# Expert loop of a decoder layer: how far ahead of a block's output each engine works on the blocks behind it

## What is computed

```
probs = softmax(x @ gate_w);  w, sel = top_k(probs, 8);  w = w / sum(w)
xg = rows of x, gathered per expert, at most C = 1024 rows each
g = xg @ w_gate[e];  u = xg @ w_up[e]            # 256 -> 96
y = (silu(g) * u) @ w_down[e]                    # 96 -> 256
out[token] += w_slot * y                         # 8 experts per token
```

## Time and profile before

| what | value |
|---|---|
| median of 3 runs | 627.1 us (624.79 to 627.71) |
| span of the profiled execution | 719.4 us |
| mean granted TensorE clock | 0.915 of full |
| busy PE / weight loads / DVE / ACT / POOL | 78 / 58 / 51 / 46 / 54 % |
| first down product to last | 390.5 to 657.6 us |

### The profile page before, as it was taken

How to read it: one execution, slowest core, us unless ns; L and a number is a source line. 1 busy time by engine, 2 the same in 40 slices (tenths; PEclk the granted TensorE clock), 3 DMA queues, 4 the chain that set the end, 5 groups by cost and what they waited for, 6 DMA issues and landing times.

```text
span 719.4 us, 17476 instructions
## 1 busy us (share of the span) xinstructions
PE 563.9 (78%) x5097; PEld 414.4 (58%) x5098; DVE 368.4 (51%) x1527; ACT 330.1 (46%) x1204; POOL 390.5 (54%) x599
## 2 busy tenths in 40 slices
PE   3768787888878888888306889988998888985995
PEld 2445454544555554444105777777777776774884
DVE  1537566666677566666402444444444444443453
ACT  2445555455455455456003555555555554553012
POOL 5443445545544455545551666766666666665432
PEclk9789999999999899999556999999999999998899
DMA  9999996111111111112285554555555454554994
GB/s 206 277 275 365 342 339 231 69 59 73 68 50 64 55 73 73 65 66 74 99 308 182 155 165 150 160 156 167 152 164 159 143 157 142 164 160 148 425 418 145
DMA packets 83069, 121.31 MB, mean 169 GB/s; under 512 B 13779, under 2 KB 72669, under 8 KB 80992
## 3 DMA queue, kind: packets, MB, share of 16 engines
q1 hardware_dynamic: 64128, 78.46, 36.3%
q0 software_dynamic: 14016, 38.44, 14.7%
q10 hardware_dynamic: 4896, 4.03, 1.7%
HBM read 56.07 MB, written 69.01 MB: 174 GB/s over the span
## 4 chain that ended last, share of the span: by engine, by line
PE 54%; issue 12%; ACT 12%; DVE 9%; DMA 6%; ACTq 3%; POOL 2%; SPq 1%; another core or an unknown queue 0%; DVEq 0%; POOLq 0%
PE bank L793 14%; PE bank L809 9%; ACT pr L870 7%; PE bank L611 5%; PE bank L785 5%; PE bank L601 4%; PE bank L803 3%; PE bank L661 3%; DMA out<-fin 3%; PE bank L744 2%; DMA wall<-results 2%; DVE nmax L1024 2%; PE bank L619 2%; ACTq L296 1%; DVE tg L1218 1%
## 5 line engine op out<-in xcount | busy, mean ns | idle before, releaser
L556 POOL DMA_INDIRECT results<-ys,wcol x152 | 150.1, 988 | 25.8 <-POOL pscrap L545 22.0
L530 POOL DMA_INDIRECT queues<-x,xidx x128 | 129.1, 1009 | 36.9 <-issue 36.5
L793 PE MATMUL bank<-wall,xtT 128*128 x616 | 127.1, 330 | 0.7 <-issue 0.7
L870 ACT ACTIVATE pr<-bank,nmax 128x128 f32<-128x128 f32 x256 | 90.9, 370 | 29.1 <-DVE nmax L1024 29.1
L1218 DVE SCALAR_TENSOR_TENSOR tg<-th,bank 128x96 f32<-128x96 f32 x154 | 39.1, 254 | 125.3 <-ACT th L957 96.9
L793 PEld LDWEIGHTS bank<-wall,xtT 128*128 128x128 f32 x616 | 98.4, 194 | 1.4 <-issue 1.3
L963 ACT ACTIVATE ys<-bank,wcol 128x256 f32<-128x256 f32 x152 | 71.9, 473 | 54.6 <-PE bank L809 36.6
L809 PE MATMUL bank<-wall,hT 96*128 x304 | 94.5, 392 | 0.0
L785 PE MATMUL bank<-ident,xt 128*128 128x128 f32 x310 | 63.3, 286 | 35.4 <-DMA xt<-queues 24.1
L785 PEld LDWEIGHTS bank<-ident,xt 128*128 128x128 f32 x310 | 59.0, 197 | 49.9 <-DMA xt<-queues 25.1
L876 ACT COPY prT<-bank 128x512 f32<-128x512 f32 x64 | 38.5, 601 | 88.9 <-PE bank L611 86.2
(11 more groups left out here) (178 smaller groups left out, 947.2 us busy)
## 6 DMA issues: line engine op xcount, KB each, us to landing
xt<-queues SPq DMA_DIRECT2D x162, 160.0 KB
results<-zeros SPq DMA_DIRECT2D x16, 1024.0 KB
wall<-results SPq DMA_DIRECT2D x16, 1024.0 KB, 12.7
queues<-zeros SPq DMA_DIRECT2D x32, 160.0 KB, 4.9
wall<-in_L_ffn_w_gate SPq DMA_DIRECT2D x4, 768.0 KB
wall<-in_L_ffn_w_up SPq DMA_DIRECT2D x4, 768.0 KB
wall<-in_L_ffn_w_down SPq DMA_DIRECT2D x4, 768.0 KB
results<-ys,wcol POOLq DMA_INDIRECT x152
```

Of the source, the lines that this page charges most:

```text
L530: pool.indirect_dma_start(xg, bass.IndirectOffsetOnAxis(ap=xidx[:, par, k:k + 1], axis=0), x2[:, par, :], None, bounds_check=last_row, oob ...
L556: pool.indirect_dma_start(yr, bass.IndirectOffsetOnAxis(ap=wcol[:, u, 1:2], axis=0), ys[:, u, :], None, bounds_check=last_y, oob_is_err=Fa ...
L793: ins = pe.matmul(bank[2 + u % 2][:, 0:2 * INTER].rearrange("p (g i) -> p g i", g=2), xtT[:, u % 2, kk, :], wall[:, bass.ds(e, GU)].rearrange(
L870: ins = act.activation(pr[:, g % 2, q, :], pS[g % 2][:, q * P:(q + 1) * P], ACT.Exp, bias=nmax[:, 4 * g + q:4 * g + q + 1], accum_out=den[ ...
```

## The change

Every step of the expert loop moves further ahead of the output, and the output's own step moves to the front of the body. For block t the body is now, on PE, `down` of t, `block_T` of t+5, `turn_h` of t+2, `gu` of t+4; on ACT the output of t, the copy of t+5, the tanh of t+4; on DVE the copy of t+2, the weights of t+3, the gate of t+4. Since `down` lags `gu` by four blocks, four offsets are carried from turn to turn. The prologue grows to five `block_T`, four `gu` and two `turn_h`, and PE's first table read moves ahead of the first `block_T`. The first eight offsets read at a turn's top are now for blocks four ahead. DVE reads its table after its first copy of a turn. SP and POOL keep their lists. Buffers and their number are unchanged.

```diff
+HALF = UN // 2
...
-            for t in range(3):
-                block_T(t, t, 0)
-            last_two = [nc.alloc_register(ET.PE, f"last_two{u}") for u in range(2)]
...
-            for t, e in zip((0, 1), neighbours(ET.PE, tab_g[0:1, LEAD:UN], (NE - 1) * WX)):
-                pe.reg_mov(last_two[t], e)
-                gu(t, t, e)
+            for r, v in zip(carried_regs, experts_of(LEAD, HALF)):
+                pe.reg_mov(r, v)
+            block_T(0, 0, 0)
+            block_T(1, 1, 0)
+            gu(0, 0, carried[0])
+            block_T(2, 2, 0)
+            gu(1, 1, carried[1])
+            block_T(3, 3, 0)
             turn_h(0, 0)
+            gu(2, 2, carried[2])
+            block_T(4, 4, 0)
+            turn_h(1, 1)
+            gu(3, 3, carried[3])
             with pe.Fori(0, rounds) as j:
-                e = neighbours(ET.PE, tab_g[0:1, bass.ds(j * UN + UN, UN)], (NE - 1) * WX)
+                e = experts_of(j * UN + (LEAD + HALF), UN)
                 for u in range(UN):
                     t = j * UN + u
-                    block_T(t + 3, u + 3, j)
-                    gu(t + 2, u, e[u])
-                    turn_h(t + 1, u + 1)
-                    down(t, u, e[u - 2] if u >= 2 else carried[u])
-                for u in range(2):
-                    pe.reg_mov(last_two[u], e[UN - 2 + u])
+                    down(t, u, e[u - HALF] if u >= HALF else carried[u])
+                    block_T(t + 5, u + 5, j)
+                    turn_h(t + 2, u + 2)
+                    gu(t + 4, u + 4, e[u])
+                for k in range(HALF):
+                    pe.reg_mov(carried_regs[k], e[HALF + k])
...
             with act.Fori(0, rounds) as j:
                 for u in range(UN):
                     t = j * UN + u
-                    block_T(t + 3, u + 3)
-                    tanh(t + 2, u)
                     y(t, u)
+                    block_T(t + 5, u + 5)
+                    tanh(t + 4, u + 4)
...
             with dve.Fori(0, rounds) as j:
-                columns = neighbours(ET.DVE, tab_w[0:1, bass.ds(j * UN + UN, UN)], D + NE - 1)
                 for u in range(UN):
                     t = j * UN + u
-                    weights(t + 2, u + 2, j, columns[u])
-                    gate(t + 2, u)
-                    h_T(t + 1, u + 1)
+                    h_T(t + 2, u + 2)
+                    if u == 0:
+                        columns = neighbours(ET.DVE, tab_w[0:1, bass.ds(j * UN + (LEAD + 3), UN)], D + NE - 1)
+                    weights(t + 3, u + 3, j, columns[u])
+                    gate(t + 4, u + 4)
```

More of the change, by code:

```diff
@@ L810, in down, with experts_of @@
                           start=True, stop=True).then_inc(peF["y"], 1)
-            for t in range(3):
-                block_T(t, t, 0)
-            last_two = [nc.alloc_register(ET.PE, f"last_two{u}") for u in range(2)]
-            carried = [bass.RuntimeValue.of_register_unchecked(r).with_bounds(min_val=0, max_val=(NE - 1) * WX) for r in last_two]
-            for t, e in zip((0, 1), neighbours(ET.PE, tab_g[0:1, LEAD:UN], (NE - 1) * WX)):
-                pe.reg_mov(last_two[t], e)
-                gu(t, t, e)
+            def experts_of(first, n):
+                return neighbours(ET.PE, tab_g[0:1, first:first + n] if isinstance(first, int)
+                                  else tab_g[0:1, bass.ds(first, n)], (NE - 1) * WX)
+            carried_regs = [nc.alloc_register(ET.PE, f"carried{k}") for k in range(HALF)]
+            carried = [bass.RuntimeValue.of_register_unchecked(r).with_bounds(min_val=0, max_val=(NE - 1) * WX)
+                       for r in carried_regs]
+            for r, v in zip(carried_regs, experts_of(LEAD, HALF)):
[6 more added lines that the diff above has]
+            block_T(3, 3, 0)
             turn_h(0, 0)
+            gu(2, 2, carried[2])
+            block_T(4, 4, 0)
+            turn_h(1, 1)
+            gu(3, 3, carried[3])
             with pe.Fori(0, rounds) as j:
-                e = neighbours(ET.PE, tab_g[0:1, bass.ds(j * UN + UN, UN)], (NE - 1) * WX)
+                e = experts_of(j * UN + (LEAD + HALF), UN)
                 for u in range(UN):
                     t = j * UN + u
-                    block_T(t + 3, u + 3, j)
-                    gu(t + 2, u, e[u])
-                    turn_h(t + 1, u + 1)
-                    down(t, u, e[u - 2] if u >= 2 else carried[u])
-                for u in range(2):
-                    pe.reg_mov(last_two[u], e[UN - 2 + u])
+                    down(t, u, e[u - HALF] if u >= HALF else carried[u])
[4 more added lines that the diff above has]
+                    pe.reg_mov(carried_regs[k], e[HALF + k])
             for b in range(NB):
@@ L968, in _ @@
                 act.copy(spare[0:1, k:k + 1], tab_n[0:1, 0:1]).then_inc(actF["y"], 1)
-            for t in range(3):
-                block_T(t, t)
-            for t in range(2):
+            block_T(0, 0)
+            for t in range(4):
+                block_T(t + 1, t + 1)
                 tanh(t, t)
@@ L1227, in h_T @@
                 dve.tensor_copy(hT[:, u % 2, :], bank[4 + u % 2][0:INTER, 0:P]).then_inc(dveF["hT"], 1)
-            for t, column in zip((0, 1), neighbours(ET.DVE, tab_w[0:1, 0:UN], D + NE - 1)[LEAD:]):
+            for t, column in zip(range(3), neighbours(ET.DVE, tab_w[0:1, LEAD:LEAD + 3], D + NE - 1)):
                 weights(t, t, 0, column)
+            gate(0, 0)
+            gate(1, 1)
             for t in range(2):
-                gate(t, t)
-            h_T(0, 0)
+                h_T(t, t)
+                gate(t + 2, t + 2)
             with dve.Fori(0, rounds) as j:
-                columns = neighbours(ET.DVE, tab_w[0:1, bass.ds(j * UN + UN, UN)], D + NE - 1)
                 for u in range(UN):
                     t = j * UN + u
-                    weights(t + 2, u + 2, j, columns[u])
-                    gate(t + 2, u)
-                    h_T(t + 1, u + 1)
+                    h_T(t + 2, u + 2)
[3 more added lines that the diff above has]
+                    gate(t + 4, u + 4)
             for u in range(UN):
```

## The result

| | before | changed |
|---|---|---|
| median of the runs | 626.9 us (4 runs) | 657.2 us (4 runs, 656.4 to 658.1) |
| ratio, 95% interval | | 1.0495 (1.0468 to 1.0521) |
| span of the profiled execution | 719.4 us (622.0 in a second profile, below) | 655.0 us |
| time of that execution | not given (623.7 for the second) | 657.0 us |

The changed kernel is 5% **slower**. The forecast was 609 us, the range 592 to 621; the time lies far outside. The two spans say the opposite, 719.4 down to 655.0. So two things need an answer: where the 30 us came from, and what the first profile of before had in it.

What follows compares the result with a forecast made beforehand. PE's array work bounds the expert loop, 214.4 us, with 52.5 us of stalls to win. Forecast 627.1 - 10 (turn's top) - 9 (second block) + 1 (prologue) = 609 us, own range 603 to 615, with rivals 592 to 621.

Steps and rivals of the forecast that it cites:

- the top's job: PE's sequencer work between a turn's last product and the next turn's first: 1.33 us before, 1.43 us after the change.
- cover of 1.58: At the turn's top, lead 0.93 us plus gate and up 0.65 us, said to hide the sequencer's job of 1.43.
- Nothing here costs array time: Claim on the longer leads in the expert loop: PE's regular block stays at 1.42 us.
- The leads: PE's tightest lead in the loop grows from 0.4 to 0.93 us; at the turn's top this gains 10 us.
- Rival 3: The longer leads don't shorten the turn's top either: 627 us, 625 to 630; chance 0.12.
- Second block, 9 us: Second block of a turn: ACT lateness of 0.8 us fits in the 0.93 lead; gain 9 us, bounds 0 and 12.5.
- sixth block, 17 us: Sixth block of a turn: stall behind a late tanh, gain 17 us at most; counted at nothing in the forecast.
- ACT's lateness at the top: ACT's late tanh just behind a turn's top, 0.8 us, counted as real because it stands at a fixed place.
- rival 2: None of ACT's lateness is real, so only the turn's top is won: 618 us; chance 0.22.
- Prologue: Ahead of the first down, PE's extra row turns, gate and up and turn_h cost +1 us, bounds 0 and 3.
- The rival on the slow side: Weights of t+3 wait for the scatter of block t-5, holding up DVE and PE: 639 us; chance 0.06.
- A sign that was there: The profiled span of 719.4 us is 92.3 over the runs' median, so stalls may exist in the profile alone.

Runs made afterwards that it cites:

- second profile: The kernel before, unchanged, profiled again: 623.7 us, one run; span 622.0 us.
- section 2: The changed kernel with PE's and DVE's tables written earlier, so both loads start at a multiple of 8 entries: 615.8 us, ratio to before 0.984.
- aligned kernel: The changed kernel with both tables shifted so PE's and DVE's turn loads start at a multiple of 8 entries: 615.8 us.
- section 6: Changed kernel with both tables aligned, PE's load later in the turn: 611.6 us; split in three: 639.6 us. Kernel before with PE's load moved: 623.8 us.
- sections 3 and 6: Kernel before, PE's load start shifted by 2 entries: 657.7 us; by 4: 626.9 us; PE's load moved behind the first turning of rows: 623.8 us.

## Why the prediction was wrong

**The step that failed is the top's job.** The prediction took the length of PE's table load over from the old trace: "a table load of 0.65" was part of a job of 1.33 us, and "Two more register moves of 0.04 and an address make it 1.43". The load became 2.14 us, and the job with it 2.9, against the prediction's cover of 1.58: a stall of 1.3 us and a restart of 0.3, where 1.5 and 0.3 were measured. The new start index stood in the diff (`LEAD + HALF` in place of `UN`): the old start was a multiple of four entries and the new one is not, and the prediction gives that no thought. The second failure is DVE's load, which was not costed at all. It went from 0.60 to 1.85 us, more than the lead of hg could take, and cost 12.6 us. "Nothing here costs array time" holds for the leads alone.

**The leads**: right in kind, and the total better than its parts. With the load as assumed, PE's waits for hg and for ACT's copy are gone, and the top went from 0.88 to 0.35 us; forecast were 0.86 and 0.3, gain 10 us, measured 626.4 - 615.8 = 10.6 (626.4 is before beside that run) with the prologue in it. Of that gain 0.22 us a turn belong to the new order, which ends a turn with the longer product, and not to the leads. The terms were off too. In before the wait that holds the sequencer is not turn_h's for hg but down's for hT: in before's second profile its step for the down starts 0.04 us behind the end of the copy of hT in 133 of 152 blocks, and at the turn's end shown in section 2 the down follows 0.31 us behind that copy, not 0.4. In the aligned kernel the last gate and up starts 0.83 us behind the end of ACT's copy, where the prediction has 0.93; the pieces it names, 0.04 + 0.37 + 0.37, make 0.78 and not 0.83, so by them it would be 0.98. The job from the end of that copy to the next down took 1.73 us, not 1.43. A stall of 0.25 was left where none was expected, and the restart behind it was 0.10 and not 0.3: two errors that nearly cancel.

Rival 3, that leads don't shorten the top, falls: at the turn's end shown, the load starts at 423.3, while the array has gate and up until 423.9. Against the Trainium skill's queue of 64 for TensorE ("Advanced Engine Details and Errata", section "Engine Queue Depths") read as a lead stand the same rows: what the sequencer is ahead is set by its next wait, 0.04 us in before and 0.36 in the aligned kernel at the branch. The runs of section 6 show the same from the other side.

**Second block, 9 us, and sixth block, 17 us**: neither shows outside the first profile. The forecast's doubt about them was right and went only half the way: it kept ACT's lateness at the top as the program's since it stood at a fixed place. The second profile has no wait of PE for hg in the loop. So the forecast of 609 us would have been 7 us too low even with fast loads; rival 2, 618 us, described the aligned kernel, 615.8, within 2.2 us. The rule that was weighed there (the Trainium skill, "Runtime: NRT & Kernel Launch", "Instruction fetch mechanics": a taken branch stalls on instruction fetch when its target is not held) would have ACT's turn without a fetch stall. The second profile agrees: ACT has no idle time without a releaser in the loop, and its longest wait for gate and up is 0.4 us. No row here shows a fetch itself.

**Prologue**: +1 forecast; the first down starts at 330.4 in the aligned kernel and at 329.3 in before's second profile, 1.1 us later. That is no proof: with the prologue of before it started at 330.7 to 331.9 in the three profiles of sections 3 and 6.

**The rival on the slow side** had the wrong mechanism. It put the danger into the scatter's return, and no wait for it shows in the loop in any trace. Its chance of 0.06 was worked out for that one mechanism, and nothing was set aside for causes that had not been thought of.

**A sign that was there**: a span 92 us above the runs. Every other profiled run here took 1.6 to 3.1 us more than its span. The gap was named and used to weigh the stalls, but the sums were still made from that execution.

## What to carry to other kernels

When a change alters an index from which a register load reads several entries, treat it as a change of alignment: shift how the table is written so that the load starts at a multiple of four 32-bit entries, and look at the load's length in the new trace. When lookahead is lengthened, the tables made for the old one go with it. A wait that no releaser explains, at the place where a sequencer loads or branches, is to be costed by what the sequencer does there, less its lead, which is the slack of its tightest wait. And where a span and the runs disagree by more than a few microseconds, no stall of that trace should carry a forecast before it is seen in a second one.

## What the runs showed of the hardware that was not expected

- A register load of eight 32-bit entries from SBUF took 0.60 us from a start at a multiple of four entries and 1.93 to 1.97 us from the others tried (1, 2, 3 and 6), measured on PE behind the loop. In the loop the slow one took 2.1 us on PE. On DVE the medians were 0.60 to 0.79 and 1.85 to 1.98.
- One such slow load a turn, 19 turns, moved a kernel of 627 us by 5%, with nothing else changed than the place of the table's entries.
- The same kernel spanned 719.4 us in one profiled execution and 622.0 in another, which took 623.7.
- PE's sequencer was held by the next wait in its list: it went on 0.04 us behind the copy of hT that it waited for in 133 of 152 blocks of before's second profile, so a longer slack of that wait is what lets it run ahead.
